# Self-attention's additions of roots on GpSimd in two halves of 256 columns, in a fused decoder block

## What is computed

```python
q, k, v = (split_heads(layernorm(x) @ W.T) for W in (Wq, Wk, Wv))        # 16 heads of 8
diff_sq = maximum(|q|^2 + |k|^2 - 2 q.k, 0)
denom   = maximum((1 - |q|^2) * (1 - |k|^2), 1e-6)
cosh    = maximum(1 + 2 * diff_sq / denom, 1)
attn    = softmax(-arccosh(cosh))                                        # over 256 keys
x       = x + (attn @ v) @ Wo.T
```

## Time and profile before

| | |
|---|---|
| median of 3 runs | 820.78 us (820.42 to 823.08) |
| profiled execution, its own time | 820.2 us |
| its span | 818.5 us |
| PE busy | 701.4 us (86%) |
| DVE busy | 648.6 us (79%) |
| ACT busy | 581.9 us (71%) |
| POOL busy | 524.2 us (64%) |

### The profile page before, as it was taken

The page is one execution under the profiler, slowest core; times in us unless marked ns, Lnnn a source line. Parts: engine busy times, 40 slices in busy tenths (PEclk is TensorE's granted clock), DMA queues, the critical chain, the costliest instruction groups (busy, mean ns, idle before and its releaser), DMA issues.

```text
span 818.5 us, 17509 instructions
## 1 busy us (share of the span) xinstructions
PE 701.4 (86%) x5760; PEld 474.6 (58%) x5760; DVE 648.6 (79%) x1643; ACT 581.9 (71%) x881; POOL 524.2 (64%) x671
## 2 busy tenths in 40 slices
PE   5456789789887787989999999999989969999996
PEld 3244455456554464545544444454436969999994
DVE  7899999999999899778888898898644845555554
ACT  4427999999999989145767866867756637776771
POOL 4518797787787796442634877876754575666663
PEclk9655555555555555658999999999987979999998
DMA  9990000000000200052061111001323122222228
GB/s 295 336 319 2 1 1 1 1 1 1 0 1 1 75 0 1 1 167 72 2 213 40 41 35 40 24 23 37 89 69 118 50 78 68 81 77 77 80 75 281
DMA packets 58152, 58.78 MB, mean 72 GB/s; under 512 B 9968, under 2 KB 49776, under 8 KB 57936
## 3 DMA queue, kind: packets, MB, share of 16 engines
q1 hardware_dynamic: 53008, 47.24, 19.4%
q0 software_dynamic: 5056, 10.43, 3.8%
HBM read 25.97 MB, written 29.57 MB: 68 GB/s over the span
## 4 chain that ended last, share of the span: by engine, by line
PE 40%; DVE 27%; issue 13%; POOL 11%; DMA 5%; SPq 2%; ACT 2%; DVEq 0%; POOLq 0%; ACTq 0%
DVE S_FB L1682 6%; PE slot L1504 5%; DVE S_YZ L1694 4%; PE ops L1397 4%; PE slot L1209 4%; PE ops L1519 3%; PE slot L1372 3%; PE ops L1232 3%; DVE S_YZ L1715 3%; PE slot L1381 3%; POOL rows L835 3%; POOL B_ROW L462 3%; PE bps L1519 2%; DVE X_junk L1745 2%; POOL picks L881 2%
## 5 line engine op out<-in xcount | busy, mean ns | idle before, releaser
L673 POOL TENSOR_TENSOR S_YZ<-S_YZ 128x512 f32<-128x512 f32 x128 | 183.0, 1463 | 57.2 <-ACT S_YZ L959 57.0
L1011 ACT ACTIVATE B_W<-slot 128x512 f32<-128x512 f32 x256 | 139.0, 595 | 79.0 <-PE slot L1381 78.9
L881 POOL DMA_INDIRECT picks<-F_ROUT,F_GOAL x94 | 103.7, 1103 | 57.3 <-DVE F_ROUT L2145 38.8
L1209 PE MATMUL slot<-S_UQT,S_UKT 32*128 32x256 f32 x256 | 84.4, 474 | 55.9 <-DVE S_YZ L1694 54.8
L1745 DVE CUSTOM_DVE_ANT_0 X_junk<-tps,X_MB 128x512 bf16<-128x512 f32 x165 | 109.9, 688 | 18.3 <-PE tps L1356 15.6
L1209 PEld LDWEIGHTS slot<-S_UQT,S_UKT 32*128 32x128 f32 x256 | 56.3, 297 | 86.1 <-DVE S_YZ L1694 71.5
L1682 DVE TENSOR_SCALAR S_FB<-slot 128x512 f32<-128x512 f32 x128 | 84.6, 683 | 13.1 <-PE slot L1213 12.5
L835 POOL DMA_INDIRECT rows<-B_ROW,B_IDX x64 | 64.6, 1009 | 31.8 <-issue 15.8
L1694 DVE SCALAR_TENSOR_TENSOR S_YZ<-slot,S_FB 128x512 f32<-128x512 f32 x128 | 83.4, 682 | 1.6
L1213 PE MATMUL slot<-S_GQT,S_GKT 32*128 32x256 f32 x256 | 84.3, 445 | 0.0
L1397 PE MATMUL ops<-B_W,X_VX 128*9 128x256 f32 x1024 | 82.4, 397 | 0.0
(11 more groups left out here) (340 smaller groups left out, 1783.2 us busy)
## 6 DMA issues: line engine op xcount, KB each, us to landing
rows<-S_blank SPq DMA_DIRECT2D x17, 1040.0 KB, 12.1
F_RIN<-rows SPq DMA_DIRECT2D x47, 130.0 KB, 2.1
B_W<-w1T SPq DMA_DIRECT2D x16, 256.0 KB, 4.8
F_W<-w2T SPq DMA_DIRECT2D x16, 256.0 KB
X_CT<-ctxT SPq DMA_DIRECT2D x8, 256.0 KB, 4.9
B_MBR<-B_MBT SPq DMA_DIRECT2D x16, 128.0 KB, 2.6
B_W<-picks SPq DMA_DIRECT2D x8, 256.0 KB, 8.7
B_W<-picks SPq DMA_DIRECT2D x4, 384.0 KB, 5.9
```

The costliest lines, as they stand in the source:

```text
L673: g.tensor_tensor(Y[:, n % YR], Y[:, n % YR], Zr[:, n % ZR], ALU.add).then_inc(f_rdy, 1)
L881: g.indirect_dma_start(out=picks[:, :], out_offset=bass.IndirectOffsetOnAxis(ap=GOAL[:, s, i:i + 1], axis=0), in_=ROUT[:, s, i, :], in_off ...
L1011: act.activation(W[:, at + i, 2 * j:2 * j + 2, :].rearrange("p t n -> p (t n)"), e_bank(k, i), ACT.Exp, scale=SCALE).then_inc(e_rdy, 1)
L1209: ins = pe.matmul(slot[n % 2][:, 0, kt * N:(kt + 1) * N], UKT[r:r + 32, p, g, kt * P:(kt + 1) * P], UQT[r:r + 32, p, g, :], start=True, st ...
```

## The change

Each addition of 512 columns is made as two of 256, on the same engine, in the same order, at the same place. Each half counts `f_rdy` up by one, so all four waits on that semaphore double their value: no one waits for less or for more work than before. POOL's wait for the root, the features between the groups, the rings and all other engines' orders are as they were. POOL issues 256 additions in the place of 128.

```diff
                 g.wait_ge(root_rdy, k + 1)
                 for n in range(R * k, R * k + R):
-                    g.tensor_tensor(Y[:, n % YR], Y[:, n % YR], Zr[:, n % ZR], ALU.add).then_inc(f_rdy, 1)
+                    for v in (slice(0, N), slice(N, 2 * N)):
+                        g.tensor_tensor(Y[:, n % YR, v], Y[:, n % YR, v], Zr[:, n % ZR, v], ALU.add).then_inc(f_rdy, 1)
...
-                    wait(act, f_rdy, R * k - ZR + R)
+                    wait(act, f_rdy, 2 * (R * k - ZR + R))
...
-                act.wait_ge(f_rdy, R * k + R)
+                act.wait_ge(f_rdy, 2 * (R * k + R))
...
-                wait(dve, f_rdy, n - ZR + 2)
+                wait(dve, f_rdy, 2 * (n - ZR + 2))
...
-            dve.wait_ge(f_rdy, B * H)
+            dve.wait_ge(f_rdy, 2 * B * H)
```

## The result

The halves made the kernel slower: 834.88 us in the median of four runs (832.41 to 841.85), against 820.73 us for the kernel before in the runs beside them, a ratio of 1.017 (95% interval 1.012 to 1.022). I had forecast 814.3 us and a range up to 821.5. The profiled execution took 837.29 us, its span is 835.5.

A forecast was written before the change was run, and what follows sets the result against it. ACT and DVE were taken to share the bound, with POOL having time to spare. Savings of 0.4 + 3.9 + 1.2 + 1.0 = 6.5 us from the 820.78 us median gave 814.3 us; range 811.0 to 821.5.

The forecast's parts named there:

- POOL's price: Self-attention adds on POOL: a half every 0.69 us, about 0.73 long; 0.14 to 0.15 us more per add, 18 us for 128.
- The slack at group 0's logarithm: ACT's logarithm after group 0's adds: 0.8 us of slack, up to 0.25 us waiting per batch, charged 0.2 x 4 = 0.8 us.
- the one on DVE's waits: Squares meeting POOL's adds wait for the one in flight, on average 0.53 us, with halves 0.26; half the waiting gone.
- had it gain 3.9: 136 to 273 us: ACT gives back 4.7 us of waits for squares, less 0.8 us at the logarithms, 3.9 us.
- Rival 2: The lock passes a waiting square by, second half going first: 8 us slower, 829 us; chance 0.10.
- My "against it": Against rival 2: behind a full add, with the next already started, the square won every time, and halves are adds too.
- A maximum of line 1715 above 2 us: Sign on the squares' line: maximum expected to fall from 2345 to about 1800 ns; above 2 us refutes the lock step.
- The last adds: 313 to 325 us: two tiny DVE operations, lines 1956 and 1957, held 2.1 us by the last adds; half, 1.0 us, saved.

The follow-up runs named there:

- the kernel of its own: Without the decoder block: one square per run of 48 halves, a copy of 64 columns every 8 halves; squares let in ahead of the next copy waited 6.56 us at most.
- the kernel with one count: The changed kernel with f_rdy counted on the second half only, 128 counts and the waits of the kernel before: 837.18 us, ratio 1.018.
- the last kernel: The changed kernel with POOL waiting for its own last half ahead of each group's first half and ahead of the features: 814.81 us, 0.991 of the kernel before.

## Why the prediction was wrong, by its own steps

- **POOL's price** was right: halves every 0.69 us, 726 ns in the median against 0.73 forecast. The page's busy time of POOL grew by 12.5 instead of 18 us; the adds' own grew by 11.1 (194.1 against 183.0), since they were held less by squares.
- **The slack at group 0's logarithm** held: in the four middle batches that logarithm never waited for POOL. The 0.8 us charged there were nothing.
- **The step that failed** is the one on DVE's waits: "whoever comes second waits for the end of the one in flight", halved with the length of an add. For a square that waits at the end of a half it is true only while POOL has fewer than some 12 to 14 instructions behind it. I took from the earlier trace rows that the square wins at each end; those rows are the 6th to 8th adds since POOL last stood still, well inside the count. Where it holds, halving did what was forecast (squares of 1.23 to 1.8 us, median 1339 ns). Six squares for which it didn't cost 27.4 us of DVE's time: 6.95 + 4 x 4.63 + 9.19 less 6 x 1.21. ACT waited 10.3 us for squares in the middle batches where I had it gain 3.9.
- **Rival 2** had the mechanism's outside and not its size or cause. It named the passing over from the cast of the earlier trace rows, and priced it as one half each time, 8 us; it is all that is left of the run, 3.4 to 8 us for one square, 14 us in all. And it read "short and close behind another" into that cast. Counted in the trace, the cast at 134.08 is the 13th instruction since POOL last stood still: the four adds from 126.33, then nine copies. I read the row as an edge of the count, not of the length; no run tests this, and for copies the edge lies elsewhere than for adds (below). In the kernel before POOL then stood still 0.58 us for PE ahead of line 667, and the square had the ports. In all it does that 8.0 us in six times:

```profile
L667 POOL CAST S_GQ<-S_QG x8: 348/582/712, 36.3 to 237.0; 128x160 fp32r<-128x160 f32 x8
...
  PE tps L1198: 8.0, 6
```

  After the change POOL comes there later and stands still once, 1.6 us. In the middle batches its run is then 8 halves, 11 copies and 8 halves without a stop, and the square of 178.0 falls into the 22nd. The square before it, of 173.36, was passed over by three copies and let in ahead of the one of 64 columns at 174.47; as in the kernel of its own, this didn't set the count back. So the change did not only double the adds, it also took away a pause that would have set it back.
- **My "against it"** for rival 2, that the halves are adds too and that an add never won twice, argued from the kind of instruction where the count decided. "A maximum of line 1715 above 2 us would make me wrong on the lock" was the right test: the maximum is 9.19 us.
- **The last adds** gave half of what I had forecast. Line 1957 (1956 before) takes 693 ns where it took 1245, for 0.6 forecast, and the next, 1958, takes 649 where it took 1187. But the two tiny operations behind them, 520 and 170 ns before, now meet a half each as well, at 650 and 650 ns: the four together take 2.75 us where they took 3.23, so 0.5 us is gained for 1.0 forecast:

```profile
L1957 DVE TENSOR_TENSOR ln_t<-ln_rs x2: 159/426/693, 336.6 to 405.1; 128x12 f32<-128x12 f32 x1, 128x4 f32<-128x4 f32 x1
```

The Trainium skill, page "SBUF — State Buffer", section "SBUF: two separate sides", has the lock held for the whole instruction. The squares agree: those of 178.0 and 292.47 end 1.08 us after the last half that they waited for, so each began its work at the end of a half. That section doesn't say which of two that wait gets the lock next, and that is where the forecast failed.

Shown is the count, that it doesn't depend on the pieces' length, that a real stop sets it back, and that breaking it takes back the change's whole loss. That a served square sets it back too is read from the trace of after alone (at 89.7 us one is served in the 23rd instruction since the last stop, the 4th since the last half that a square held; the one of 115.3 us loses in the 14th since such a half) and from that of the kernel with one count (one is served in the 42nd since the last stop, the 5th since such a half); one in the 21st, at 104.6 us, comes 9 instructions behind a copy that a square held; no run takes it apart. In the features of the kernel with a wait ahead of every second head squares lost one end in the 8th instruction, near a tie, and three in a row from the 11th on, so the count is not the same for every form. What in the chip counts is open. Open too is why the kernel before gains 1.0% by waits ahead of whole adds, when none of its runs in the loop lose squares to adds: its squares wait 8.3 us less, and I take it, not shown, that the two engines then fall otherwise against each other. Whole adds with the few stops of the last kernel, which would tell what the halving adds, were not run.

## What to carry to other kernels

Where VectorE and GpSimd share SBUF ports, don't count only how long a GpSimd instruction is, but how many follow one another without a stop: cutting one into pieces is safe for VectorE only while the row stays at 12 instructions or fewer (for copies perhaps fewer still). A wait of GpSimd for its own last instruction (0.12 us, one for every 8) keeps it there; a wait that is fulfilled already does not. And measure the waits without the cutting too: here they gained as much by themselves. Look at the maximum beside the median of the VectorE line, and for a single length that equals the rest of GpSimd's run.

## What the runs showed of the hardware that I had not expected

- A square (VectorE, two SBUF inputs) that starts while GpSimd is in the 16th or later of back-to-back adds waits until the run ends or nearly so: 215 of 215, up to 23.40 us; one from the 15th took 24.06. Up to the 13th it was served at the next end 315 times of 315, a tie aside; three more from the 13th, in the changed kernel, in the one with one count and in a kernel of its own, lost to the end of the run.
- It goes by instructions (0.41, 0.68 or 1.22 us apiece) and not by time. A copy of 64 columns within the run lets a waiting square in and, once squares lose, doesn't set the count back.
- Back-to-back adds come every 0.276, 0.410, 0.545, 0.680, 0.949 and 1.219 us for 64, 128, 192, 256, 384 and 512 columns: 2.1 ns a column and 0.14 us apiece. A wait for the engine's own last instruction adds 0.12 us, where I had expected 0.05 to 0.1; one that is fulfilled already adds nothing.
